# Loop: down projections wait for the state input's fifth-last product with five instructions, their last twelve products for the state's first output

## The reference

```python
x = x + attn(layernorm(x))      # below
x = x + ffn(layernorm(x))

# attn
xp, z = jnp.split(x @ w_in, 2, axis=-1)          # 512 each
xc = silu(causal_conv4(xp) + conv_b)
h = h * 0.9 + 0.1 * (xt @ w_B)                   # scan over time, 16 states
y = (h @ w_C) * silu(z)
out = y @ w_out

# ffn: experts idx = top_k(x[:, 0] @ Wr + br, 2)
h = gelu(x @ W1[idx] + b1[idx])
out = sum over the two of (h @ W2[idx] + b2[idx]) / 2
```

## Time and profile before

| | us |
|---|---|
| three runs | 505.78, 505.89, 507.0 (median 505.89) |
| the profiled execution | 505.8 |
| its span, first to last instruction | 504.0 |
| PE busy | 498.7 (99%) |
| PE weight loads busy | 440.4 (87%) |
| DVE busy | 452.9 (90%) |
| ACT busy | 400.2 (79%) |
| POOL busy | 348.7 (69%) |

### The profile page before, as it was taken

One profiled execution on the slowest core, in us unless ns is written; L12 is line 12 of the kernel. 1 busy time (PEld: TensorE's weight loads), 2 busy tenths in 40 slices (PEclk: granted clock), 3 DMA queues, 4 the chain that ended last, 5 costly groups with the idle time before them and its releaser, 6 DMA issues.

```text
span 504.0 us, 9945 instructions
## 1 busy us (share of the span) xinstructions
PE 498.7 (99%) x3026; PEld 440.4 (87%) x3026; DVE 452.9 (90%) x896; ACT 400.2 (79%) x692; POOL 348.7 (69%) x390
## 2 busy tenths in 40 slices
PE   8999999999999999999999999999999999999997
PEld 7888799788888988888888888988889888888997
DVE  6999999989998899989999899998999989996773
ACT  4986959878869788697887969779797888969554
POOL 4959597559693696928969197782977649764291
PEclk9999999999999999999999999999999999999999
DMA  8940105344151532605235160432604333130102
GB/s 259 298 179 6 37 1 179 114 142 153 64 190 42 167 125 83 208 10 199 82 125 166 42 221 28 165 126 83 208 31 136 125 126 126 47 120 1 42 2 85
DMA packets 53380, 57.29 MB, mean 114 GB/s; under 512 B 8682, under 2 KB 49642, under 8 KB 53226
## 3 DMA queue, kind: packets, MB, share of 16 engines
q1 hardware_dynamic: 51498, 56.67, 33.7%
q10 hardware_dynamic: 1856, 0.31, 0.3%
HBM read 35.46 MB, written 21.50 MB: 113 GB/s over the span
## 4 chain that ended last, share of the span: by engine, by line
PE 98%; DVE 1%; DMA 1%; issue 0%; DVEq 0%
PE blk L1299 16%; PE blk L1302 16%; PE blk L1308 16%; PE tok L1422 12%; PE tok L1424 12%; PE tok L1423 11%; PE blk L1510 3%; PE turn L1489 3%; PE turn L1486 3%; PE turn L1246 1%; PE tok L1308 1%; PE tok L1302 1%; PE tok L1299 1%; DMA x_mid<-in_L_attn_x 1%; DVE stats_t L917 0%; DVE normed L934 0%
## 5 line engine op out<-in xcount | busy, mean ns | idle before, releaser
L992 DVE SCALAR_TENSOR_TENSOR conv<-blk,tap_w,conv 128x512 f32<-128x512 f32 x192 | 130.1, 742 | 7.2 <-ACT conv L683 6.3
L488 POOL TENSOR_TENSOR y_lo<-gate,y_hi 128x512 fp32r<-128x512 f32 x57 | 72.2, 1297 | 35.9 <-ACT y_hi L611 35.8
L1299 PE MATMUL blk<-xn_hi,w_in_hi 128*128 128x512 f32 x228 | 89.6, 393 | 0.0
L1302 PE MATMUL blk<-xn_hi,w_in_lo 128*128 128x512 f32 x228 | 89.0, 390 | 0.0
L453 POOL TENSOR_TENSOR xc_lo<-conv,xc_hi 128x512 fp32r<-128x512 f32 x60 | 73.2, 1236 | 7.5 <-ACT xc_hi L611 7.4
L1422 PE MATMUL tok<-w_out_hi,y_hi 128*128 128x256 f32 x256 | 71.1, 278 | 0.0
L1423 PE MATMUL tok<-w_out_lo,y_hi 128*128 128x256 f32 x256 | 70.8, 276 | 0.0
L1424 PE MATMUL tok<-w_out_hi,y_lo 128*128 128x256 f32 x256 | 70.7, 276 | 0.0
L1308 PE MATMUL blk<-xn_lo,w_in_hi 128*128 128x512 f32 x228 | 70.4, 390 | 0.0
L1422 PE MATMUL tok<-w_hi,hid_hi 128*128 128x256 f32 x248 | 69.8, 281 | 0.2
L1424 PE MATMUL tok<-w_hi,hid_lo 128*128 128x256 f32 x248 | 69.3, 279 | 0.0
(11 more groups left out here) (189 smaller groups left out, 1320.5 us busy)
## 6 DMA issues: line engine op xcount, KB each, us to landing
spill<-normed SPq DMA_DIRECT2D x25, 512.0 KB, 2.9
normed<-spill SPq DMA_DIRECT2D x100, 128.0 KB, 2.8
out<-x_mid SPq DMA_DIRECT2D x30, 256.0 KB, 2.4
x_mid<-in_L_attn_x SPq DMA_DIRECT2D x29, 256.0 KB, 2.8
x_in<-in_L_attn_x SPq DMA_DIRECT2D x14, 512.0 KB, 3.8
w_all<-in_L_ffn_W SPq DMA_DIRECT2D x2, 2048.0 KB, 11.3
b_all<-in_L_ffn_b SPq DMA_DIRECT2D x1, 1024.0 KB, 13.9
gate<-in_L_attn_w_in SPq DMA_DIRECT2D x2, 256.0 KB, 4.8
```

What stands on the lines that cost most here:

```text
L488: nc.gpsimd.tensor_tensor(y_lo[:, j, :], gate_of(o, j), y_hi[:, j, :].bitcast(F32), ALU.subtract).then_inc(y_lo_set, 1)
L992: nc.vector.scalar_tensor_tensor(cols, blk[j][:], tap_w[:, j, t:t + 1], cols, ALU.mult, ALU.add).then_inc(tap_added, 1)
L1299: ins = mm(dst, whi(k), his(k), start=(k == 0), stop=False)
L1302: mm(dst, wlo(k), his(k), start=False, stop=False)
```

## The change

In the loop alone, two things are added or replaced. First, ahead of the 36 down products, `behind_next(state_tail, ...)` gives way to `behind_fifth(state_fifth, ...)`. The new semaphore `state_fifth` is raised by two when the last `xc_hi` product of the state input ends, which is the fifth-last of the eight. The helper is an increment, an addition to the threshold, an increment that carries the wait, two more increments, an addition, and an increment that carries the wait for the next value (there already). Second, ahead of the last 12 down products a `behind_next` is added that waits for the first of the four state outputs, through `c_ready`, whose threshold moves by four a step.

```diff
--- before.py
+++ after.py
@@ -173,6 +173,7 @@
 
 
         passed = sem("passed")
+        state_fifth = sem("state_fifth")
         x_tail, state_tail, up_tail = sem("x_tail"), sem("state_tail"), sem("up_tail")
         paced = sem("paced")
 
@@ -1237,8 +1238,10 @@
         def _(pe):
             mm = nc.tensor.matmul
             x_nth, state_nth = nc.tensor.alloc_register("x_nth"), nc.tensor.alloc_register("state_nth")
+            c_nth = nc.tensor.alloc_register("c_nth")
             nc.tensor.reg_mov(x_nth, FIRST + 1)
-            nc.tensor.reg_mov(state_nth, FIRST + 1)
+            nc.tensor.reg_mov(c_nth, FIRST * JD + 1)
+            nc.tensor.reg_mov(state_nth, 0)
 
             def turns(normed, sem_out):
                 for k in range(KD):
@@ -1430,12 +1433,23 @@
                 for _ in range(PACE):
                     pe.sem_inc(paced, 1)
 
-            def behind_next(tail, nth):
+            def behind_next(tail, nth, step=1):
                 pe.sem_inc(paced, 1)
                 pe.wait_ge(tail, nth)
                 for _ in range(PACE - 1):
                     pe.sem_inc(paced, 1)
+                nc.tensor.reg_add(nth, nth, step)
+
+            def behind_fifth(tail, nth):
+
+                pe.sem_inc(paced, 1)
                 nc.tensor.reg_add(nth, nth, 1)
+                pe.wait_ge(tail, nth)
+                for _ in range(PACE):
+                    pe.sem_inc(paced, 1)
+                nc.tensor.reg_add(nth, nth, 1)
+                pe.wait_ge(tail, nth)
+                pe.sem_inc(paced, 1)
 
             def down_tile(f, n, dst, js=range(JF)):
                 rows = slice(n * P, (n + 1) * P)
@@ -1457,7 +1471,7 @@
                         if isinstance(f, int):
                             behind(*tail)
                         else:
-                            behind_next(state_tail, state_nth)
+                            behind_fifth(state_fifth, state_nth)
                     t, cols = j // KD, slice(j % KD * D, (j % KD + 1) * D)
                     ins = tokens(h, j, j == JF - 1, hid_hi, hid_lo, w2_hi[:, t, cols], w2_lo[:, t, cols])
                 if js[-1] == JF - 1:
@@ -1483,7 +1497,9 @@
                 bank = u_bank(a)
                 for j in range(JD):
                     pe.wait_ge(xc_hi_set, a * JD + j + 1)
-                    mm(bank[:], b_mix[:, j, :], xc_hi[:, j, :], start=(j == 0), stop=False)
+                    ins = mm(bank[:], b_mix[:, j, :], xc_hi[:, j, :], start=(j == 0), stop=False)
+                if not isinstance(a, int):
+                    ins.then_inc(state_fifth, 2)
                 for j in range(JD):
                     pe.wait_ge(xc_lo_set, a * JD + JD if isinstance(a, int) and a < 3 else a * JD + j + 1)
                     ins = mm(bank[:], b_mix[:, j, :], xc_lo[:, j, :], start=False, stop=(j == JD - 1))
@@ -1629,6 +1645,8 @@
                     state_out(a, s)
                 if isinstance(s, int) and s == LAST:
                     turns2(LAST - 1)
+                if not isinstance(a, int):
+                    behind_next(c_ready, c_nth, JD)
                 down(f, 1, (2, 3))
 
             opening()
```

## The result

The changed kernel takes 507.48 us (median of 14 runs, 506.75 to 508.04), the kernel before 506.58 in the same sittings (14 runs, 505.78 to 507.12). The ratio is 1.0016, with a 95% interval of 1.0009 to 1.0023: about 0.8 us slower, clear of noise and within the 0.3% that I called no change. 506.6 and +0.8 were forecast. The difference is what came out as forecast; the time itself lies 0.9 above the forecast, mostly because the kernel before has 506.58 in these 14 runs and had 505.89 in the three that the forecast started from. The profiled execution of the change took 506.75, its span 504.9 against 504.0.

The account below looks back on a forecast made before the run. PE was taken to bound the kernel, busy for 98% of the span. Odd steps -0.50, even steps +1.32 and last twelve 0 gave +0.8 on 505.8, so 506.6 us, range 505.1 to 507.6.

Parts of the forecast that it names:

- Even steps, late by the sequence: In even steps the longer queue sequence behind the hidden split delays the first down product; +1.32 us in all.
- a sign of being wrong: In PE's queue: an addition or an increment cheaper than 0.1 us would show the forecast wrong.
- the old stalls: PE's existing stalls in step 6, 0.09 at the second x product and 0.06 in the state output, offset lateness.
- DVE holding the even steps: DVE's multiplication by the gate opens the next x block in even steps, so a faster PE wins nothing there.
- Odd steps: In odd steps the first down load, 0.07 ahead of its product, brings the fast pace: 0.10 each, 0.50 in all.
- Last twelve: The new wait ahead of the last 12 down products costs nothing and wins nothing: 0.
- the first rival: Both the 36 and the last twelve down products catch the fast pace, -0.54 more: +0.3, 506.1 us; chance 0.20.
- the x block behind each odd step: The loop's end and next x block's waits, queued behind the last twelve, are covered by their 1.4 us: no cost.

Follow-up runs that it names:

- e1: The change without the wait ahead of the last twelve, so only the fifth-last wait ahead of the 36 down products; 1.0021 to the kernel before, 507.03 us.
- e3: The change with the fifth-last wait in odd steps only, the old fourth-last wait in even steps; 0.9990 to the kernel before, 505.49 us.
- e7: The whole change with two more increments at the head of the sequence in even steps; 1.0051 to the kernel before, 508.57 us.
- e8: e3 with no sequence ahead of the 36 down products in even steps; 1.0005 to the kernel before, 506.05 us.
- e9: e8 with DVE's first multiplication by the gate moved ahead of the tokens' low parts in the loop's even steps; 0.9997 to the kernel before, 505.71 us.
- e10: e3 with DVE's first multiplication by the gate moved ahead of the tokens' low parts in even steps; 0.9987 to the kernel before, 505.32 us.
- e11: e2 with DVE's first multiplication by the gate moved ahead of the tokens' low parts in even steps; 0.9985 to the kernel before, 505.09 us.
- e4: The whole change with the fifth-last sequence ahead of the wait for the hidden split, not behind it; 1.0004 to the kernel before, 506.02 us.
- e2: The kernel before plus only the new wait ahead of the last twelve, the old fourth-last wait kept; 0.9995 to the kernel before, 505.75 us.
- e5: The kernel before without the loop's two sequences, ahead of the out projections and of the down products; 1.0042 to the kernel before, 508.26 us.

## Why the prediction was right, and where it wasn't

**Even steps, late by the sequence: right.** Forecast was 0.90 from the released increment to the load, and the trace has 0.86, since an addition took 0.09 and not 0.11. (The prediction named anything under 0.1 as a sign of being wrong; here it moves a step by 0.04.) The first product was to be 0.39 and 0.32 later in steps 6 and 12 and was 0.30 and 0.29 later. The five sum to +1.50. Since the block of 36 stayed about where it was (-0.07) and the old stalls gave back 0.25 (forecast: 0.30), the even steps cost +1.18 against +1.32. e1, e3 and e7 show it: alone it slows the kernel, without it the change is a gain, and two more increments cost 0.3 a step.

**DVE holding the even steps: right.** The prediction calls DVE's work in step 6 unbroken, which it isn't quite: up to 195.18 DVE waited 0.20 for ACT's part of the state. The rest holds. The stall of 0.09 at the second x product went away where PE came later, came back in e8 and vanished in e9, e10 and e11 when the multiplication was moved.

**Odd steps: right in size, loose in the reason.** -0.45 against -0.50. Four blocks won 0.13 with the load 0.15 behind the last state product, and one, in step 5, lost 0.06: there one increment took 0.18 in place of 0.15 and the load stood at 0.175. The prediction took a place between two fast ones, 0.10 and 0.04 ahead of the product, for fast; step 5's load was 0.05 ahead and its block slow. Nine profiles (this kernel's two, e1, e3, e4, e7, e8, e9 and e10) have the fifth-last wait in odd steps: all 27 blocks with the load at 0.145 took 4.11 to 4.13, all 18 with 0.175 took 4.29 or 4.30. Four of five had the good place in the change, two to four of five in the others; what decides between the two is open, so the size of this term was partly luck.

**Last twelve: wrong.** The step that failed is "the load would come 0.10 after the fourth starts, a shade earlier than the 0.11 that left step 5 slow ... I expect it to win nothing." The load did come at 0.10, and all ten blocks were fast at once: -0.50, close to the first rival's 0.54. I had made a rule of four places of a load, and e2 shows the same place with the other pace. What it gave was partly taken again by the x block behind each odd step (0.026 each, +0.13), which I had put at nothing: with the queue emptied 1.4 us before the loop's end, the loop's branch is passed later. By the trace it is passed 2.6 us before the x block behind step 7 in the kernel before and 1.5 us before it with the change. The loss itself comes with part two: the profiles of all kernels that have it show +0.12 to +0.14 here, those of e1 and e5 without it 0.01 at most. That the later branch is the reason was only argued.

**What made up for it: luck.** The written-out steps 14 to 17 cost 0.51 more in this profile, which I hadn't looked at, as their code is the same. 0.21 of that was an execution's own (down blocks, gone in the second profile). 0.30 was there in both, 0.22 of it in step 14's out projections, whose first load came 0.16 behind the last product instead of 0.13. Why the loop's change moves it stays open; e8 and e9 have it too, e4, with both parts, hasn't. So the sum of +0.8 was met by two errors of opposite sign beside the terms that held: -0.37 for part two, +0.3 to +0.5 outside the loop. Nothing in the prediction made them cancel.

One comparison of the prediction says less than it seems to. It sets the trace's 113 and 118 ns against the 109 of the Trainium skill, "TensorE: Matmul & The Clock Gate", section "Back-to-back issue gap". The section calls this formula the gap of an isolated matmul, and says that in a stream of pairs of weight load and matmul, as here, both set the spacing. So 113 and 118 don't test it. No term of the sum used it.

## What to carry to other kernels

Count what stands in the queue behind each wait, and ask which wait is released last: a sequence that is free behind an early operand costs its full length behind a late one, here in every second step. Where a two-step loop has one step held by another engine, a gain in that step is lost until the other engine's last piece is moved, so move that first. And a pattern seen in a few places of one profile, such as the pace of a block, should be looked for in a second profile of the same kernel before a rule is made of it.

## What the runs showed of the hardware

The same 256-column products run at 0.1133 or 0.1177 us each for a whole block, and which of them a block gets depends on how the queue stood at its start: with nothing emptied it was always the slower (e5, all 20 blocks of the loop's out projections and 36 down products), with the queue emptied just before, it depends on the block. Over the loops of all 14 profiles, 128 of 130 such blocks of out projections, 92 of 100 such blocks of twelve and 64 of 120 such blocks of 36 were fast. Some change between executions of one kernel.

With the fifth-last wait in odd steps, a load at 0.145 behind the last state product was followed by the fast pace and one at 0.175 by the slow one, in 45 blocks without an exception. Across kernels the place isn't enough: a load 0.11 behind the last state product was followed by 4.24 us for the 36 in the two profiles of the kernel before and in e11 (14 blocks), and by 4.08 in e2, e3 and e10 (7 blocks). In the profiles of e1, e2, e3, e7 and e10 the loop's out projections take 5.456 us where most others have 5.440, and each of these profiled executions was slower than the median of its kernel, by 0.3 to 1.4 us. Whether this goes with the program or with the execution, no run here tells.

An increment in PE's queue takes 0.15 us and now and then 0.18, an addition 0.09 to the next increment and 0.06 to a weight load.
